# Last graph-attention layer: head scores taken from the layer's input by TensorE, and the first head started inside the second weight matrix

## What is computed

```python
h = (x @ W).reshape(n, heads, out_c)            # x: 625x768, W: 768x768, 8 heads of 96
al_s = jnp.einsum('nhc,hc->nh', h, a_src)       # one number per node and head
al_d = jnp.einsum('nhc,hc->nh', h, a_dst)
e = leaky_relu(al_s[src] + al_d[dst], 0.2)      # then a softmax over the edges of each dst
out[dst] = sum(alpha * h[src])                  # then + bias, elu, and a second layer of one head
```

## Time and profile before

| | |
|---|---|
| median of 3 runs | 1712.84 us (1711.83 to 1715.08) |
| the profiled execution | 1712.94 us, its span 1711.1 us |
| PE busy | 1522.8 us, 89% |
| DVE busy | 842.0 us, 49% |
| ACT / POOL busy | 595.1 / 530.1 us |
| chain of work that ended last | PE 60%, DVE 13%, issue 10% |

### The profile page before, as it was taken

One profiled execution on the slowest core, in us unless ns is written; L12 is line 12 of the kernel. 1 busy time (PEld: TensorE's weight loads), 2 busy tenths in 40 slices (PEclk: granted clock), 3 DMA queues, 4 the chain that ended last, 5 costly groups with the idle time before them and its releaser, 6 DMA issues.

```text
span 1711.1 us, 26859 instructions
## 1 busy us (share of the span) xinstructions
PE 1522.8 (89%) x10084; PEld 1472.3 (86%) x10084; DVE 842.0 (49%) x2112; ACT 595.1 (35%) x1183; POOL 530.1 (31%) x675
## 2 busy tenths in 40 slices
PE   4988999998879999987999999999999998867787
PEld 3757889997879889986999999999999998757787
DVE  5886776316467763265522313141231315489843
ACT  3335444323345542232322232222223031257721
POOL 3235233233333242233213232323235131133322
PEclk9989999999989999988899999999999999868898
DMA  2222111122211111233112122112132222101122
GB/s 89 83 77 62 34 48 44 50 81 87 81 49 39 38 48 50 67 108 103 33 31 62 48 60 63 54 54 62 37 89 82 83 74 91 46 22 35 34 74 92
DMA packets 88989, 105.50 MB, mean 62 GB/s; under 512 B 9689, under 2 KB 80840, under 8 KB 88861
## 3 DMA queue, kind: packets, MB, share of 16 engines
q1 hardware_dynamic: 72850, 75.06, 15.0%
q10 hardware_dynamic: 16011, 28.73, 5.2%
HBM read 88.12 MB, written 11.78 MB: 58 GB/s over the span
## 4 chain that ended last, share of the span: by engine, by line
PE 60%; DVE 13%; issue 10%; ACT 6%; DMA 5%; POOL 4%; DVEq 1%; ACTq 0%; POOLq 0%; SPq 0%
PE ps L860 36%; PE ps L1070 7%; PE ps L956 5%; PE ps L1052 4%; DVE junk L1942 3%; DVE prob L1993 3%; PE ps L913 2%; DMA xl<-x_scratch 2%; PE ps L1091 2%; PE ps L1114 1%; DMA xl<-in_x 1%; POOL pairs L1204 1%; DVE prob L2001 1%; PE ps L883 1%; ACT pairs L1293 1%
## 5 line engine op out<-in xcount | busy, mean ns | idle before, releaser
L1204 POOL TENSOR_TENSOR pairs<-stage,pairs 128x256 fp32r<-128x256 f32 (+2 forms) x466 | 367.0, 805 | 790.9 <-ACT pairs L1293 789.8
L860 PE MATMUL ps<-pairs,XB 128*125 128x256 f32 (+2 forms) x2760 | 403.8, 307 | 26.4 <-issue 15.0
L860 PEld LDWEIGHTS ps<-pairs,XB 128*125 128x125 f32 (+1 forms) x2760 | 392.6, 193 | 30.0 <-issue 16.7
L860 PE MATMUL ps<-pairs,XA 128*125 128x256 f32 (+3 forms) x2505 | 357.0, 303 | 6.4 <-DVE XA L1626 2.3
L1293 ACT ACTIVATE pairs<-stage 128x256 fp32r<-128x256 f32 (+2 forms) x466 | 185.7, 423 | 508.0 <-PE ps L860 383.2
L860 PEld LDWEIGHTS ps<-pairs,XA 128*125 128x125 f32 (+1 forms) x2505 | 351.1, 188 | 8.4 <-issue 2.8
L1626 DVE TENSOR_TENSOR Hl<-ps,Hl 125x768 fp32r<-125x768 f32 (+3 forms) x57 | 43.6, 818 | 270.8 <-ACT Hl L1345 270.8
L956 PE MATMUL ps<-AT,Hg 125*128 125x314 f32 (+1 forms) x1080 | 168.9, 317 | 3.8 <-DVE rl L2030 3.8
L956 PEld LDWEIGHTS ps<-AT,Hg 125*128 125x128 f32 (+1 forms) x1080 | 163.9, 193 | 4.8 <-DVE rl L2030 3.7
L1251 POOL TENSOR_SCALAR prob<-prob,rden 125x625 f32<-125x625 f32 x80 | 78.1, 977 | 214.6 <-DVE rden L2009 214.6
L913 PE MATMUL ps<-ident,prob 125*125 125x125 f32 x475 | 85.8, 324 | 43.7 <-POOL prob L1251 18.7
(11 more groups left out here) (226 smaller groups left out, 1685.0 us busy)
## 6 DMA issues: line engine op xcount, KB each, us to landing
stage<-in_W SPq DMA_DIRECT2D x210, 128.0 KB, 2.3
stage<-in_rel SPq DMA_DIRECT2D x99, 192.0 KB, 2.4
stage<-in_root SPq DMA_DIRECT2D x91, 64.0 KB, 1.8
x_scratch<-xo ACTq DMA_DIRECT2D x15, 375.0 KB
xl<-x_scratch ACTq DMA_DIRECT2D x15, 375.0 KB
stage<-in_rel SPq DMA_DIRECT2D x42, 128.0 KB, 2.1
stage<-in_root SPq DMA_DIRECT2D x12, 192.0 KB, 2.4
stage<-in_W SPq DMA_DIRECT2D x12, 192.0 KB, 2.4
```

Source lines behind the costliest of these rows:

```text
L860: last = mm(o, X[:rows, xi, a, P * (s0 + t):P * (s0 + t) + m], pair(n, b), start=k == 0 and i == 0 and t * pitch % BANK == 0, stop=k == le ...
L1204: nc.gpsimd.tensor_tensor(pair(n, 1), staged(n), pair(n, 0).bitcast(F32), ALU.subtract).then_inc(*up("weights_lo", "weights lo", n))
```

## The change

1. The sixteen vectors W·a (8 heads, source and target) are made on chip. During layer 2's last part W1 is loaded once more, whole (2.36 MB), with both attention vectors (0.39 MB each) on ACT's DMA queue, into space of `XB` that is free then (`w1x`, `a1x`). DVE makes 96 multiply-and-sums of 96 columns (`score_weights`, in six batches of 16, each behind a `rows_lo` of the relations) and splits the result to a pair `vpair` (`score_pairs`).
2. `score_cols` on PE: for each node tile 18 matmuls of 16 columns, `XB` stationary, into one PSUM bank. Tiles 0 to 2 stand ahead of `early`, tile 3 behind it, tile 4 behind the last `norm_T`. `score_cols_in` on DVE copies all 80 columns out and scales the target scores, two operations for all heads.
3. The `dots` and `score_sum` of layer 3's first half go. The attention vectors of that half are no longer loaded to `ab`.
4. `spread` and `scores` of head 0 come before the first matrix's last 30 matmuls. The loop starts before `rows_lo` of the first matrix (now t == 1), and the second matrix is laid into the loop: one k tile at each of t = 3, 4 and 5, two at t = 6, the last at t = 7, with `rows` and `rows_lo` behind it. It holds its five banks from t = 3 to t = 7.
5. The pre-splitting of weights follows: `rows` of a layer-3 projection no longer triggers it, `split` and `split_to` steps do.

```diff
@@ gat_steps, l == 3
-        yield ("project", l, 0, 384)
-        yield from rows_of(("project", l, 0, 384))
-        yield ("part", ("project", l, 1, 384), 0, 2)
-        yield from (("score_sum", l, 0), ("spread", l, 0), ("scores", l, 0), ("mask_rows", l, 0, 0))
-        yield ("project", l, 1, 384)
-        yield ("split", ("project", l, 1, 384), 1)
+        first, second = FIRST_MATRIX[3], ("project", l, 1, 384)
+        yield from (("spread", l, 0), ("scores", l, 0), ("mask_rows", l, 0, 0))
+        yield from (("split", first, 4), first, ("rows", first), ("split", first, 6))
...
-                if d == 1 and h + 1 < heads:
-                    yield ("score_sum", l, h + 1)
...
-            if t == 2:
-                yield from rows_of(("project", l, 1, 384))
+            if t == 1:
+                yield ("rows_lo", first)
+            if 3 <= t < 7:
+                yield ("part", second, t - 3, 5 if t == 6 else t - 2)
+            if t == 4:
+                yield ("split", second, 1)
+            if t == 7:
+                yield from (second, ("rows", second), ("rows_lo", second))
+            if 9 <= t < 24 and t % 3 == 0:
+                yield ("split_to", ("project2", l, 0, 256), t // 3 - 2)
...
-            if d == 2 and h + 1 < heads:
+            if d == (2 if h else 3) and h + 1 < heads:
                 yield ("spread", l, h + 1)
@@ rgcn_steps
+WEIGHTS_AFTER = {(0, 1): (0,), (0, 2): (1,), (1, 0): (2, 3), (1, 1): (4,), (1, 2): (5,)}
+                    for k in WEIGHTS_AFTER.get((c, r), ()):
+                        yield ("score_weights", k)
+                    if (c, r) == (1, R - 1):
+                        yield ("score_pairs",)
...
+    for d in range(NT - 2):
+        yield ("score_cols", d)
     yield ("early", first)
+    yield ("score_cols", NT - 2)
     yield from normalized(3, NT - 1)
+    yield ("score_cols", NT - 1)
+    yield ("score_cols_in",)
     yield ("late", first)
     yield ("split", first, 1)
@@ PE
+                elif kind == "score_cols":
+                    d = s[1]
+                    if d == 0:
+                        q = acquire("score_cols", banks=1)
+                        held.add(place[q])
+                        pe.wait_ge(*at("v lo"))
+                    q = fill_of["score_cols",]
+                    pe.wait_ge(*at("input lo", 3, d))
+                    for k in range(6):
+                        for i, (a, b) in enumerate(PASSES):
+                            last = mm(slot(q)[:P, 16 * d:16 * d + 16], XB[:128, k, a, P * d:P * d + P], vpair[:, b, k, :],
+                                      start=d == 0 and k == 0 and i == 0, stop=k == 5 and i == 2, skip_group_check=True)
@@ ACT, graph_load
-                    load_vectors(len(gat_projects) - 5)
+                    act.dma_start(w1x[:, :, :], I["W1_3"].rearrange("(k p) c -> p k c", p=128)).then_inc(
+                        *up("w1_in", "W1 in", by=16))
+                    for v, name in enumerate(("a1src_3", "a1dst_3")):
+                        act.dma_start(a1x[:, v, :], I[name].partition_broadcast(128)).then_inc(
+                            *up("w1_in", "W1 and vectors in", by=16))
@@ DVE
+                elif kind == "score_weights":
+                    k = s[1]
+                    dve.wait_ge(*at("W1 and vectors in"))
...
+                            V.tensor_tensor_reduce(
+                                out=junkx[:, j % 2, :], in0=w1x[:, k, 96 * h:96 * h + 96], in1=a1x[:, v, 96 * h:96 * h + 96],
```

More of the change, by code:

```diff
@@ L487, in split_limit @@
                 used = wend[s]
-            elif s[0] == "rows" and s[1][0] == "project" and s[1][1] < 3:
+            elif s[0] == "rows" and s[1][0] == "project":
                 return 0
@@ L513, in build @@
                    "graph_out1", "graph_in", "degrees_out", "degrees_in"]
-                + [f"counts_back{d}" for d in range(NT)] + [f"counts_in{d}" for d in range(NT)] + ["att_lo_act", "minus_one"] + [f"x2_moved{h}" for h in range(GAT_HEADS[3][0])])
+                + [f"counts_back{d}" for d in range(NT)] + [f"counts_in{d}" for d in range(NT)] + ["att_lo_act", "minus_one", "w1_in", "v_dot", "v_pair"] + [f"x2_moved{h}" for h in range(GAT_HEADS[3][0])])
         sems = {n: ctx.enter_context(nc.semaphore(n)) for n in names + dmas}
@@ L899, in _ @@
                     hb = heads_order[s[1:]] % 2
+                    column = asp[:, 0, s[2], :] if s[1] == 3 and s[2] < GAT_HEADS[3][0] else asad[:, hb, 0, :]
                     for j in range(NT):
                         last = nc.tensor.transpose(slot(q)[:P, 128 * j:128 * j + P],
-                                                   asad[:, hb, 0, j:j + 1].to_broadcast([P, P]), ident[:P, :P])
+                                                   column[:, j:j + 1].to_broadcast([P, P]), ident[:P, :P])
                     last.then_inc(*up("psum_filled", "filled", *s))
@@ L1319, in load_vectors @@
                 if i >= 2:
-                    act.wait_ge(*at("vectors read", i - 2))
+                    last_layer = gat_projects[i - 2][:2] == ("project", 3)
+                    act.wait_ge(*at("vectors read", i - 4 if last_layer else i - 2))
                 w = s[3]
@@ L1461, in _ @@
                         if l == 3 and h < 2:
-                            act.wait_ge(*at("filled", "rows", ("project", 3, 1, 384), 2))
+                            act.wait_ge(*at("filled", "rows", ("project", 3, h, 384), 2))
                         elif l == 3:
@@ L1919, in _ @@
                         last.then_inc(*up("lo_ready", "rows lo", s, g))
-                        if kind == "relation" or s[:1] == ("project2",) and s[2] == 2:
+                        if kind == "relation" or s[:1] == ("project2",) and s[2] == 2 or s[:2] == ("project", 3):
                             G.same(("rows lo", s, g), "free", q)
@@ L1953, in _ @@
                         G.same(("dot", junks[0] - 1), "dots", s)
+                elif kind == "score_weights":
+                    k = s[1]
+                    dve.wait_ge(*at("W1 and vectors in"))
+                    for h in range(8):
+                        for v in range(2):
+                            j = 16 * k + 2 * h + v
+                            if j >= 2:
+                                dve.wait_ge(*at("v dot", j - 2))
+                            V.tensor_tensor_reduce(
+                                out=junkx[:, j % 2, :], in0=w1x[:, k, 96 * h:96 * h + 96], in1=a1x[:, v, 96 * h:96 * h + 96],
+                                scale=1.0, scalar=0.0, op0=ALU.mult, op1=ALU.add,
+                                accum_out=vv[:, k, 8 * v + h:8 * v + h + 1]).then_inc(*up("v_dot", "v dot", j))
+                elif kind == "score_pairs":
+                    dve.wait_ge(*at("v dot", 95))
+                    V.tensor_copy(vpair[:, 0, :, :], vv[:, :, :]).then_inc(*up("v_pair", "v hi"))
+                    dve.wait_ge(*at("v hi"))
+                    minus_hi(vpair[:, 1, :, :], vv[:, :, :], vpair[:, 0, :, :]).then_inc(*up("v_pair", "v lo"))
+                elif kind == "score_cols_in":
+                    q = fill_of["score_cols",]
+                    dve.wait_ge(*at("filled", "score_cols"))
+                    V.tensor_copy(asp[:, :, :, :].rearrange("p v h t -> p t (v h)"),
+                                  slot(q)[:P, :16 * NT].rearrange("p (t c) -> p t c", t=NT)).then_inc(
+                        *up("scores_step", "all scores"))
+                    G.same(("all scores",), "free", q)
+                    dve.wait_ge(*at("all scores"))
+                    V.tensor_scalar(ad8w[:, :, :], asp[:, 1, :, :], 1 - SLOPE, None, ALU.mult).then_inc(
+                        *up("scores_step", "all target scores"))
+                    for h in range(GAT_HEADS[3][0]):
+                        G.same(("all scores",), "scores col", 3, h)
+                        G.same(("all target scores",), "target scores", 3, h)
                 elif kind == "part_sum":
```

22 lines of the change are left out of this document (16 added, 6 removed).

## The result

| | before | changed |
|---|---|---|
| median (5 runs each) | 1712.84 us | 1723.62 us, ratio 1.0046 [1.003, 1.0062] |
| later, with the experiments (19 and 8 runs) | 1715.65 us | 1724.43 us, ratio 1.0048 [1.0032, 1.0063] |
| profiled execution, its span | 1712.94, 1711.1 us | 1721.18, 1719.3 us |

The account below looks back on a forecast made before the run. PE bounds the kernel on average, DVE the last layer's head loop, with time lost there waiting for dots. A lead of 8.3 us after Stage C plus 1.0 gave 9.3 off 1712.94: 1703.6 us, range 1697 to 1714.

Parts of the forecast that it names:

- Stage A: Layer 3's start up to the first `mask_rows`, with the 90 small matmuls: lead of 11.0 us over the kernel before.
- Layer 2, at nothing: Layer 2's last part: W1's load and six batches of dots stay hidden and cost nothing, 4 us to spare.
- I take 105: Layer 3's small matmuls: 105 ns each, from a row with two columns, so 9.5 us for 90.
- my upper bound: Layer 3's small matmuls: 210 ns each, the row's price at half clock, 18.9 us for 90.
- Stage B: First `mask_rows` to `score_rows` of tick 3, the dots gone: lead grows from 11.0 to 21.5 us.
- Stage C: Ticks 3 to 8, second matrix laid in, one PSUM slot serving in turn: lead falls from 21.5 to 8.3 us.
- Stage D: From t = 9, less DVE work a head but five weight splits in the loop: 1.0 us gained, bounds 1.8 and -1.
- their 72 GB/s: Layer 2's last part: its own weights need 72 GB/s of 273, leaving 200 for the W1 load, landing at 1299.
- Rival 3: Layer 2: W1 lands late and DVE, then PE, wait; 1715.2 us at half the load rate; chance 0.14.
- Rivals 1 and 2: Layer 3: small matmuls at 53 ns, 1698.9 us, chance 0.2; PE's clock low in stage C, 1713.8 us, chance 0.16.

Follow-up runs that it names:

- the run with one pass: Changed kernel with only one of the three passes of small matmuls, 30 instead of 90, low parts left out of the scores; ratio 0.9991 to the kernel before.
- The run with the exponential first: Changed kernel with ACT's read-out of the first matrix and its two splits moved behind the first tick's exponential; ratio 1.0034 to the kernel before.
- the run with the second matrix whole: Changed kernel with the second matrix computed whole ahead of the loop and read out at t == 2; ratio 1.0018 to the kernel before.
- the storage alone: Kernel before with the change's two small buffers and three semaphores allocated but never used; ratio 0.9998.

## Why the prediction was wrong

The first traces differ by +8.2 us of span where I had summed -9.3: 17.5 us. Two steps of the prediction failed: the price of the small matmuls in stage A, and layer 2 "at nothing".

- **Stage A, 7.4 us.** The term that failed is "I take 105": the small matmuls cost 15.1 us (17.2 in the second trace), so 5.6 (7.7) more. The price was right, the clock was not: 1.88/18 = 104 ns at clock 1.00, 11.36/54 = 210 ns at 0.50, just my upper bound. I had kept 210 as a bound of the price and given no case of its own to the clock's being low under these very matmuls. The rest is the `late` part behind them, which the low clock takes in too (4.0 us for 2.6), and 0.4 up to `mask_rows`. That all this reaches the end is shown by the run with one pass: 9.9 us of small matmuls less, 10.1 us of time less (9.8 by the medians' ratios).
- **Stage B, right.** Forecast 10.5 us of gain, measured 10.3, with the reciprocal released by the exponential and `rows_lo` behind it. The run with the exponential first puts this delay at 2 to 4 us to the end; I had described it and not asked what it was worth.
- **Stage C, right in size.** Forecast -13.2, measured -14.1, with PE nearly full and waiting for read-outs of the one PSUM slot (1.69 us ahead of `spread`, while DVE's low part waited 2.72 us for ACT's high part). I should have asked whether a step that gives back 13 of 21 us is worth its place: the run with the second matrix whole is faster by 3.7 to 7. Some 2 to 4 us of that can be the late exponential, which that order avoids too. With the exponential first and the scores made cheap the two orders can't be told apart. What part the one slot has and what part PE's work between the transposes was not separated.
- **Stage D.** +1.0 forecast, -0.4 measured; within the scatter of the fourth distance (181.4 to 184.4).
- **"Layer 2, at nothing", 3.2 us** (4.2 as the mean of six traces with this load against three without). The last byte came at 1299.0, which is my number by luck: in this trace the layer began 4.4 us later, so from there on the load was 4.4 us faster than forecast. The step that failed is the division of the bandwidth: I gave the weights their 72 GB/s first and W1 the rest. It was the other way: ACT's queue took 3.73 MB and SP's 1.0 MB in 18 us, and a weight tile took 7.7 us to land. The wait left its mark on the clock as well: PE's next 78 matmuls took 15.5 us, and 14.0 where it had not waited. The Trainium skill, page "DMA: Bandwidth & Descriptors", section "Queues, rings and completion order", says that each DMA engine takes turns between queues packet by packet. The trace does not bear out what I drew from it, that neither is shut out: from 1284 to 1290 us SP's queue moved nothing, with loads issued from 1286.0 on. Why is not shown. Rival 3 had this place, with W1 as the one that comes late.
- **4.4 us ahead of everything** in the first pair of traces is scatter, as the storage alone (7 us later with the same code) and the repeated runs show.
- Rivals 1 and 2 fell. The mechanism that came true, small matmuls at half clock together with starved weights, had no chance of its own; I had split it over two bounds. The range ended at 1714, the price of one bad term, where two came together.

The idea itself holds: the dots leave the path and the head starts earlier. What spoils it is how the scores are formed and where W1 is loaded. With the operands exchanged, the load moved and one of the two orders mended, it gives 0.8%.

## What to carry to other kernels

A matmul with few moving columns costs its stationary load, so put the narrow operand on the stationary side and let the long one move, even if a transpose has to follow. When a change adds work to an engine that is the bound, price that work at both clock levels and give the low one a chance. A bulk load is hidden only if the DMA engines have room at its place: look for what else is loaded then, not only for when the load itself must be there.
